# Cross-attention: context products behind the scores, softmax first on VectorE, square splits first on GpSimd; opening, last chunk and root re-ordered

## The reference, cut to what matters

```python
x = x + tanh(g_xattn) * xattn(layernorm(x), ctx, Wq, Wk, Wv, Wo, gq, gk)
x = x + tanh(g_ffn) * ffn(layernorm(x), ...)

# xattn
q = rmsnorm(hidden @ Wq, gq); k = rmsnorm(ctx @ Wk, gk); v = ctx @ Wv
attn = softmax(q @ k.T / sqrt(128))
out = (attn @ v) @ Wo

# ffn: rmsnorm, causal self-attention with residual, rmsnorm, then
probs = softmax(t @ gate_w.T); the 6 best of 16 experts, weights renormalised
out = sum_e cw_e * (silu(t @ eg_e.T) * (t @ eu_e.T)) @ ed_e.T + one shared expert
```

## Time and profile before

| what | value |
|---|---|
| median of 3 runs | 696.73 us (695.54 to 697.88) |
| the profiled execution: time, span | 695.13 us, 693.3 us |
| PE busy | 673.0 us, 97% of the span |
| DVE, ACT, POOL busy | 66%, 49%, 44% |
| DMA | 16 engines, 71 GB/s read over the span |

### The profile page before, as it was taken

How to read it: one execution, slowest core, us unless ns; L and a number is a source line. 1 busy time by engine, 2 the same in 40 slices (tenths; PEclk the granted TensorE clock), 3 DMA queues, 4 the chain that set the end, 5 groups by cost and what they waited for, 6 DMA issues and landing times.

```text
span 693.3 us, 14660 instructions
## 1 busy us (share of the span) xinstructions
PE 673.0 (97%) x5422; PEld 586.7 (85%) x5422; DVE 458.9 (66%) x881; ACT 341.6 (49%) x688; POOL 304.0 (44%) x372
## 2 busy tenths in 40 slices
PE   8799999999899999999999999999999999999997
PEld 6588878888787898999889889998888888888886
DVE  4567777769666666676665758865555888655555
ACT  4567667567665334524344523345446644444443
POOL 4534433534333243433333335334554566655553
PEclk9999999999999999999999999999999999999999
DMA  6511221110101123221212212111332332333332
...
DMA packets 35850, 50.08 MB, mean 72 GB/s; under 512 B 4048, under 2 KB 22864, under 8 KB 35792
## 3 DMA queue, kind: packets, MB, share of 16 engines
...
## 4 chain that ended last, share of the span: by engine, by line
PE 85%; DVE 6%; ACT 4%; POOL 3%; issue 2%; DMA 0%; SPq 0%; DVEq 0%; POOLq 0%; ACTq 0%
PE acc L539 20%; PE bank_k L512 15%; PE bank_q L512 14%; PE bank_v L613 7%; PE bank_v L512 5%; PE bank_s L659 5%; PE bank_s L512 4%; PE bank_p L680 2%; PE bank_p L645 2%; PE bank_q L634 2%; POOL sq_k_lo L1455 2%; PE bank_p L690 2%; PE bank_t L690 2%; PE bank_t L667 2%; ACT sq_q L901 1%
## 5 line engine op out<-in xcount | busy, mean ns | idle before, releaser
L539 PE MATMUL acc<-wo_hi,pv_hi 128*128 128x256 f32 x328 | 94.6, 288 | 2.1 <-DVE pv_lo L1325 1.5
L1455 POOL TENSOR_TENSOR sq_k_lo<-sq_k,sq_k_hi 128x512 fp32r<-128x512 f32 x32 | 48.6, 1518 | 102.7 <-ACT sq_k_hi L910 102.7
L539 PE MATMUL acc<-wo_lo,pv_hi 128*128 128x256 f32 x328 | 92.6, 282 | 0.0
L539 PE MATMUL acc<-wo_hi,pv_lo 128*128 128x256 f32 x328 | 92.2, 281 | 0.0
L1455 POOL TENSOR_TENSOR wq_lo<-raw_m,wq_hi 128x256 fp32r<-128x256 f32 x50 | 44.1, 883 | 59.9 <-DVE wq_hi L1283 55.7
L906 ACT ACTIVATE kt<-bank_k 128x512 f32<-128x512 f32 x64 | 38.3, 598 | 64.0 <-PE bank_k L512 64.0
L539 PEld LDWEIGHTS acc<-wo_hi,pv_hi 128*128 128x128 f32 x328 | 61.5, 188 | 6.4 <-DVE pv_lo L1325 2.4
L539 PEld LDWEIGHTS acc<-wo_lo,pv_hi 128*128 128x128 f32 x328 | 61.8, 188 | 1.8
L539 PEld LDWEIGHTS acc<-wo_hi,pv_lo 128*128 128x128 f32 x328 | 62.0, 189 | 0.0
L984 ACT ACTIVATE pv_hi<-rows_t 128x512 fp32r<-128x512 f32 x50 | 31.6, 632 | 61.2 <-DVE rows_t L1321 59.5
L1325 DVE TENSOR_TENSOR pv_lo<-rows_t,pv_hi 128x512 fp32r<-128x512 f32 x50 | 37.1, 743 | 36.0 <-ACT pv_hi L984 36.0
...
## 6 DMA issues: line engine op xcount, KB each, us to landing
...
```

What stands on the lines that cost most here:

```text
L539: last = nc.tensor.matmul(acc[t // 2][:, (t % 2) * D:(t % 2 + 1) * D], w[:, tok], m, start=begins and n == 0, stop=True, skip_group_check= ...
L1455: nc.gpsimd.tensor_tensor(lo, raw, hi, ALU.subtract).then_inc(signal, 1)
```

## The change

No arithmetic changes. These are moved:

- In `cross_pair` on PE, `context_values(prev)` comes directly behind `scores(u)`, and the keys of the next pair's second head come behind the queries of its first. With it, ACT copies `rows_t` at the end of the pair's own body and not at the start of the next, takes the context values ahead of the keys, and does the exponentials ahead of all squares.
- In `cross_pair` on DVE, `subtract_max` comes ahead of `split_context_values(prev)`, `normalise` ahead of the next pair's queries and weight casts, and `split_value_out` ahead of the piece in the second slot.
- In `cross_pair` on POOL, both square splits come ahead of the weight splits of the pair after next.
- The opening: three idle products in place of ten, the second head's keys ahead of all queries, the first half of `ctxt_lo` on DVE in place of POOL, the squares of both keys ahead of those of the queries.
- The last chunk: the hidden values are multiplied, rounded and split in two halves of 256 tokens, and PE starts on the first half; the last accumulator is added in two parts, the last two token tiles are stored by two transfers, one from SP and one from ACT.
- The table of the experts' pieces starts one chunk earlier and leaves a chunk free between `best` and `weights`; `root` on ACT runs ahead of `split_hidden(nxt)`.

```diff
--- before.py
+++ after.py
@@ -90,6 +91,11 @@
         return self.pair * 16 + 16
+
+    def parts(self, tokens):
+
+        count = 2 if self.final else 1
+        return [(slice(p * tokens // count, (p + 1) * tokens // count), self.done() + p) for p in range(count)]
@@ -163,7 +169,8 @@
         for n, name in enumerate(names.split()):
-            pieces["m", half, start + n, 0] = (name, step)
+            if name != "-":
+                pieces["m", half, start + n, 0] = (name, step)
@@ -175,8 +182,8 @@
                  ties=(4, 0), better=(4, 1), ranks=(5, 0), best=(5, 1), weights=(6, 0), spread=(pairs - 1, 0))
-    experts = "sums root scale turn logits equals ties better ranks best weights spread"
-    beside_chunks(0, chunks - 14, experts, ("t", 1))
+    experts = "sums root scale turn logits equals ties better ranks best - weights spread"
+    beside_chunks(0, chunks - 15, experts, ("t", 1))
     beside_chunks(0, chunks - 2, "blend", ("t", 0))
@@ -497,8 +505,9 @@
                     sp.wait_ge(out_ready, 2 * half + b + 1)
-                    sp.dma_start(out_v[half, :, 2 * b:2 * b + 2], xs[:, half, 2 * b:2 * b + 2]).then_inc(st_out, 16)
-            sp.wait_ge(st_out, 16 * 2 * HALVES)
+                    two = slice(2 * b, 2 * b + 1 if half and b else 2 * b + 2)
+                    sp.dma_start(out_v[half, :, two], xs[:, half, two]).then_inc(st_out, 16)
+            sp.wait_ge(st_out, 16 * (2 * HALVES + 1))
@@ -555,9 +564,11 @@
             def output_chunk(u):
-                pe.wait_ge(M["hh_lo"], u.done())
                 pe.wait_ge(M["wd_lo"], u.done())
-                add_output(u, u.parity, wo_hi[u.parity][:], wo_lo[u.parity][:]).then_inc(M["down"], 1)
+                for tiles_of, number in u.parts(NT):
+                    pe.wait_ge(M["hh_lo"], number)
+                    last = add_output(u, u.parity, wo_hi[u.parity][:], wo_lo[u.parity][:], tiles_of)
+                last.then_inc(M["down"], 1)
@@ -737,22 +748,16 @@
                 scores(u)
+                if prev:
+                    pe.wait_ge(A["ln_k"], u.n)
+                    context_values(prev)
                 if nxt.kind == "a":
...
                     project_keys(nxt, 0)
-                else:
-                    pe.wait_ge(A["ln_q"], u.n)
-                    project_queries(nxt, 0)
-                if prev:
-                    pe.wait_ge(A["ln_k"], u.n)
-                    context_values(prev)
-                if nxt.kind == "a":
-                    project_keys(nxt, 1)
-                    pe.wait_ge(A["ln_q"], u.n)
-                    project_queries(nxt, 0)
-                else:
-                    project_keys(nxt, 0)
+                pe.wait_ge(A["ln_q"], u.n)
+                project_queries(nxt, 0)
+                project_keys(nxt, int(nxt.kind == "a"))
                 if prev:
@@ -823,11 +828,11 @@
             project_keys(start, 0)
-            for _ in range(WARM_UP // 2):
+            for _ in range(SETTLE):
                 nc.tensor.matmul(bank_s[:], zeros[:, 0:P], zeros[:], start=True, stop=True)
-            project_queries(start, 0)
             project_keys(start, 1)
-            project_queries(start, 1)
+            for h in range(2):
+                project_queries(start, h)
             norm_k(start)
@@ -976,37 +981,33 @@
             def split_hidden(u):
-                act_e.wait_ge(M["hh"], u.done())
                 if u.in_first_pair:
...
                     act_e.wait_ge(M["down"], u.done(2))
-                nc.scalar.activation(pv_hi[:, u.parity], hh, ACT.Copy).then_inc(M["hh_hi"], 1)
+                for part, number in u.parts(HT):
+                    act_e.wait_ge(M["hh"], number)
+                    nc.scalar.activation(pv_hi[:, u.parity, part], hh[:, part], ACT.Copy).then_inc(M["hh_hi"], 1)
...
                 prev, nxt = u.prev(), u.next()
-                if prev:
-                    take_rows(prev)
                 root_k(u)
...
                 root_q(u)
-                if nxt.kind == "a":
-                    take_k(nxt, 0)
-                    square_k(nxt, 0, sq_k, A["sq_k"])
                 if prev:
                     take_context_values(prev)
+                take_k(nxt, 0)
+                exponentials(u)
                 if nxt.kind == "a":
+                    square_k(nxt, 0, sq_k, A["sq_k"])
+                    square_k(nxt, 0, sq_k_hi, A["sq_k_hi"])
                     take_k(nxt, 1)
-                    square_k(nxt, 0, sq_k_hi, A["sq_k_hi"])
+                    square_k(nxt, 1, sq_k, A["sq_k"])
+                    square_k(nxt, 1, sq_k_hi, A["sq_k_hi"])
                     square_q(nxt, 0)
-                else:
-                    take_k(nxt, 0)
-                exponentials(u)
                 prepare(u)
                 if nxt.kind == "a":
-                    square_k(nxt, 1, sq_k, A["sq_k"])
-                    square_k(nxt, 1, sq_k_hi, A["sq_k_hi"])
                     square_q(nxt, 1)
@@ -1014,8 +1015,8 @@
                     log_k(nxt)
-                else:
-                    take_rows(u)
+                take_rows(u)
+                if nxt.kind != "a":
                     take_v(nxt, False)
@@ -1069,9 +1070,13 @@
                     split_up(after, u.done())
+                early = piece_at(u)[0] == "root"
+                if early:
+                    prepare(u)
                 if nxt:
                     split_hidden(nxt)
-                prepare(u)
+                if not early:
+                    prepare(u)
@@ -1093,11 +1098,14 @@
                 square_k(start, h, sq_k_hi, A["sq_k_hi"])
+            for h in range(2):
                 square_q(start, h)
...
                 run_units(act_e, kind, half, bodies[kind])
+            act_e.wait_ge(out_ready, 2 * HALVES + 1)
+            act_e.dma_start(out_v[HALVES - 1, :, NT - 1], xs[:, HALVES - 1, NT - 1]).then_inc(st_out, 16)
@@ -1318,11 +1326,14 @@
                     v.wait_ge(M["hh_hi"], u.done(1))
-                nc.vector.tensor_tensor(hh, up_bank(u)[:], gu, ALU.mult).then_inc(M["hh"], 1)
+                for part, _ in u.parts(HT):
+                    nc.vector.tensor_tensor(hh[:, part], up_bank(u)[:, part], gu[:, part], ALU.mult).then_inc(M["hh"], 1)
             def split_hidden(u):
-                v.wait_ge(M["hh_hi"], u.done())
-                nc.vector.tensor_tensor(pv_lo[:, u.parity], hh, pv_hi[:, u.parity], ALU.subtract).then_inc(M["hh_lo"], 1)
+                for part, number in u.parts(HT):
+                    v.wait_ge(M["hh_hi"], number)
+                    nc.vector.tensor_tensor(pv_lo[:, u.parity, part], hh[:, part], pv_hi[:, u.parity, part], ALU.subtract)\
+                        .then_inc(M["hh_lo"], 1)
@@ -1337,12 +1348,14 @@
                     if kind == "b":
-                        add = nc.vector.tensor_tensor(ys[:, half, two], part, ys[:, half, two], ALU.add)
-                    else:
-                        gate = tg[:, 0:1] if kind == "a" else tg[:, 1:2]
-                        add = nc.vector.scalar_tensor_tensor(xs[:, half, two], part, gate, xs[:, half, two],
-                                                             ALU.mult, ALU.add)
-                    add.then_inc(out_ready if kind == "m" else acc_free, 1)
+                        nc.vector.tensor_tensor(ys[:, half, two], part, ys[:, half, two], ALU.add).then_inc(acc_free, 1)
+                        continue
+                    gate = tg[:, 0:1] if kind == "a" else tg[:, 1:2]
+                    singly = kind == "m" and half == HALVES - 1 and b == 1
+                    for own in ((slice(0, 1), slice(1, 2)) if singly else (slice(0, 2),)):
+                        into = xs[:, half, two][:, own]
+                        nc.vector.scalar_tensor_tensor(into, part[:, own], gate, into, ALU.mult, ALU.add)\
+                            .then_inc(out_ready if kind == "m" else acc_free, 1)
                 if kind != "m":
@@ -1351,15 +1364,15 @@
                 scale_scores(u)
+                subtract_max(u)
                 if prev:
                     split_context_values(prev)
-                subtract_max(u)
                 if nxt.kind == "b":
                     split_values(nxt)
+                normalise(u)
                 take_q(nxt, 0)
...
                 split_keys(after, 0, nxt)
-                normalise(u)
                 prepare_piece(*piece_at(u), u)
@@ -1368,9 +1381,9 @@
                 split_keys(after, 1, nxt)
-                prepare_piece(*piece_at(u, 1), u)
                 if u.weighs_values:
                     split_value_out(u)
+                prepare_piece(*piece_at(u, 1), u)
@@ -1436,6 +1449,8 @@
                                            ALU.mult, ALU.mult).then_inc(setup_dve, 1)
+            v.wait_ge(ctxt_hi_ready, 1)
+            nc.vector.tensor_tensor(ctxt_lo[:, 0:HT], ctxt[:, 0:HT], ctxt_hi[:, 0:HT], ALU.subtract).then_inc(ctxt_lo_ready, 1)
             v.wait_ge(setup_act, 1)
@@ -1506,12 +1521,14 @@
```

(19 more changed lines are left out.)

8 lines of the change are left out of this document (5 added, 3 removed).

## The result

The changed kernel took 690.01 us (median of 4 runs, 689.21 to 692.05), the kernel before 697.31 beside it (4 runs, 695.54 to 698.38): a ratio of 0.990, 95% interval 0.988 to 0.992. The profiled execution took 690.55 us, span 688.8, against 695.13 and 693.3. I had said 692.0 for the median and 690.4 for the profiled execution. So the profiled executions lie 4.6 us apart and the medians 7.3, where I had forecast 4.7 for both.

The account below looks back on a forecast made before the run. PE, busy 97% of the span, was taken as the bound. Opening 4.2, pairs -0.5, last chunk 0.9 and experts 0.1 summed to 4.7 us won: 690.4 us profiled, 692.0 median, range 687.5 to 695.0.

Parts of the forecast that it names:

- The opening: Start of the kernel through pair 0: shorter PE waits and scores at full clock, 4.2 us won.
- Half 0: Cross-attention pairs of half 0: a new PE wait for `pv_lo` at `output`, 7 x 0.23 = 1.6 us lost.
- the old `vo_lo` wait: Cross-attention: the 1.1 us wait goes, but the `norm` piece delays the next pair by about as much: 0.
- The rival of the free wait: Cross-attention pairs: fewer tiling changes and `pv_lo` in time, 7.6 us in place of -0.5, 683.9 in all; chance 0.12.
- Half 1: Cross-attention pairs of half 1: waits for squares go, new `pv_lo` waits come, net 1.1 us won.
- Experts and root: Experts' stage: moved pieces and early `root`, whose delay of one `pv_hi` PE could absorb; 0.1 us won.
- The last chunk: End of the kernel: split hidden values remove the 0.80 us wait, last transfer half as large; 0.9 us won.
- The clock: Rival in the opening: PE's clock falls again after its idle stretches, 3.1 us won in all, 693.6; chance 0.24.
- The sum: Whole kernel: all terms together, 4.7 us won, 690.4 us profiled and 692.0 us for the median.

Follow-up runs that it names:

- e5: Changed kernel with the first half of `ctxt_lo` moved back from VectorE to GpSimd, between the splits of the two heads; profiled span 690.9 us.
- e4: Changed kernel with `pv_lo` ahead of `subtract_max` on VectorE and, on ACT, the exponentials behind the first head's squares; median 683.87 us.
- e3: Changed kernel with two lines on VectorE swapped back, so `pv_lo` comes ahead of `subtract_max` in each cross-attention pair; median 695.08 us.
- e12: Kernel before with only TensorE's `cross_pair` order taken from the changed kernel; half-0 pairs of 13.92 us.
- e1: Changed kernel with `root` on ACT put back behind `split_hidden`; median not distinguishable from the changed kernel's.
- e7: Changed kernel with the last chunk's hidden values whole again, the last store still split over two queues; profiled span 688.6 us.
- e2: Changed kernel with `root` put back behind `split_hidden` and the old table of experts' pieces; median not distinguishable from the changed kernel's.
- e6: Changed kernel with `cross_pair` as before on all four engines, the other changes kept; median 695.48 us.

## Why the prediction was right, and where it was not

**The opening** was right in kind. PE waited 0.55, 0.94 and 1.55 us (for the squares, for `kt`, for the squares) for 0.7, 1.0 and 1.9 predicted, and the scores ran at full clock. It was worth 5.3 in these two profiles and not 4.2, with the scatter of about 0.5 either way that the starts of pair 0 have (see e5). I charged 0.75 us for `ctxt_lo` on VectorE and placed the first `norm_k` at 17.9; it came at 16.73. The mis-sized term is that charge: VectorE's `ctxt_lo` took its usual 0.68, and it was GpSimd's `wq_lo` beside it that took 1.32. I had also not looked at what `ctxt_lo` did where it was: it held up `hn` (e5), and without it the first keys started at 10.78 for 11.37. The charge and these 0.6 us together are 1.35, and `norm_k` came 1.2 earlier than I said.

**Half 0** was right. `output` starts 6.40 us into the pair (61.99 − 55.59) for 6.41 predicted, with a wait in the foreseen 0.2 to 0.4, and the period is 13.07 for 12.83 + 0.23. The pairs lost 1.2 for 1.6, for the pair of the old `vo_lo` wait became 0.2 shorter (14.64 for 14.86) and not longer.

**The rival of the free wait** had its mechanism right, which e4 shows: without waits a pair of half 0 takes 12.57, not 12.83. The keys that stood alone between scores and context products took 0.90 us (141.14 to 142.04 in the trace of before) for three steps of 0.23, so that stop cost 0.2. In the changed kernel the wait for `pv_lo` hides this gain.

**Half 1** was mis-sized: I said 1.1 net, and 2.6 was measured, 2.3 of it up to the last pair. I counted idle time as shown. In the trace of before the pair's last `output` product starts at 149.51; such products follow each other in 0.12, so `norm_k` could start at 149.63 and started at 150.11. That is 0.48, and `norm_k` and the transposes behind it took 1.55 us instead of 1.46: 0.57 for 0.32 shown. In the same way the 0.25 shown for `pv_lo` costs 0.50 (12.21 against e4's 11.70). Two more runs with TensorE's order of e4 agree: e3's half 1 shows 0.67 and takes 0.94 longer (12.64), e12's half 0 shows 1.10 and takes 1.35 longer (13.92 against 12.57).

**Experts and root** was the step that failed: "0.1 us won", "PE has more than that in hand there". The profile shows 2.7 us lost: 1.3 by the early `root` and 1.2 by the clock that fell behind it (e1 and e7); 0.4 won by the table and some 0.65 lost that I haven't placed (e2) leave the other 0.2. I counted the delay of one `pv_hi` and not that `scale` and GpSimd's splits would come together, though the earlier trace rows show such a collision. The fall of the clock here stood in none of my terms.

**The last chunk** won 0.6 against the kernel before and 0.75 against e7, for 0.9 predicted: the shorter wait, and nothing from the smaller last transfer.

**The clock.** The 0.24 for a fall in the opening was fair. Of the six profiles with both of pair 0's waits as in the changed kernel it fell in two, e2 and e3, between 26 and 36 us, though e1, e2 and the changed kernel have the same waits there (e6, with the longer wait, fell too, from 28 to 40 us). What decides it in one execution stays open.

**The sum** came out by luck: the errors cancelled. The terms gave 1.1 and 1.5 too little for the opening and half 1 and 0.4 too little for half 0, and 2.8 and 0.3 too much for experts and last chunk. The median had an error of its own. I had added 1.6 us to the profiled time because the median of before lay that much above it; the changed kernel's median lies 0.5 below its profiled execution. Its four executions have mean clocks of 0.995 to 1.000, two of them 1.000, while none of the more than forty executions of the kernel before that were timed beside the experiments is above 0.998. So part of what the change wins in the median is clock, which I had counted only in the scores of the opening.
